# One inverse root for eight pairs of tiles, and no negated mean, in the main loop of a cross-attention and ternary feed-forward kernel

## What is computed

```python
x = x + xattn(layernorm(x), ctx_1024, Wq, Wk, Wv, Wo)   # x: (64, 512, 512), ctx: (64, 77, 512)
x = x + ffn(layernorm(x), weight, bias)
# layernorm: (x - m) / sqrt(v + eps), no learned scale
# xattn: 16 query heads of 32 summed to 4 key heads, rope on q and k, softmax over 77,
#        out.mean over the 4 heads, then @ Wo
# ffn: ternary weight; i_scale = max|x| / 127 over the whole input, x rounded to -128..127, matmul, scales, bias
```

## Time and profile before

| | us |
|---|---|
| median of 3 runs | 1320.01 (1319.31 to 1321.22) |
| the profiled execution, its own time | 1319.5 |
| its span in the profile | 1317.7 |
| busy time: PE, PEld | 1267.9, 1085.9 |
| busy time: DVE, ACT, POOL | 1181.8, 1025.1, 791.2 |

### The profile page before, as it was taken

The page is one execution under the profiler, slowest core; times in us unless marked ns, Lnnn a source line. Parts: engine busy times, 40 slices in busy tenths (PEclk is TensorE's granted clock), DMA queues, the critical chain, the costliest instruction groups (busy, mean ns, idle before and its releaser), DMA issues.

```text
span 1317.7 us, 36811 instructions
## 1 busy us (share of the span) xinstructions
PE 1267.9 (96%) x9848; PEld 1085.9 (82%) x9911; DVE 1181.8 (90%) x2772; ACT 1025.1 (78%) x2338; POOL 791.2 (60%) x1536
## 2 busy tenths in 40 slices
PE   5897999999999999999999999999969999999998
PEld 5796999999999999999999999999935555555554
DVE  4876899999999999999999999999978888888887
ACT  3454788888888888888888888888857878888886
POOL 3564888888888888888888888888820000000000
PEclk9999999999999999999999999999979999999999
DMA  8574355555555555555546452323108999999945
GB/s 266 166 216 133 107 158 182 154 183 161 176 165 171 165 171 167 170 171 166 178 159 187 150 169 76 102 80 98 37 5 332 400 401 395 401 399 404 406 201 223
DMA packets 100815, 265.18 MB, mean 201 GB/s; under 512 B 49705, under 2 KB 65769, under 8 KB 72114
## 3 DMA queue, kind: packets, MB, share of 16 engines
q1 hardware_dynamic: 100786, 264.86, 58.8%
HBM read 139.64 MB, written 125.17 MB: 201 GB/s over the span
## 4 chain that ended last, share of the span: by engine, by line
DVE 47%; PE 31%; issue 15%; DMA 2%; DVEq 2%; SPq 1%; ACT 1%; POOL 1%; POOLq 0%; ACTq 0%
PE bank L1248 18%; DVE amax L898 10%; DVE x_sb L930 8%; DVE e_sb L944 6%; DVE mx_sb L940 5%; DVE bn_sb L889 5%; PE bank L1239 4%; PE bank L1246 3%; DVE qT_sb L912 2%; PE bank L1065 2%; DVE rinv_sb L886 2%; DVE ve_sb L918 2%; DVE bn_sb L881 2%; DVE mv_sb L904 1%; DMA x_sb<-in_ctx 1%
## 5 line engine op out<-in xcount | busy, mean ns | idle before, releaser
L1248 PE MATMUL bank<-wT,x_sb 128*128 128x512 f16 x1024 | 263.9, 380 | 3.5 <-issue 0.2
L1168 PE MATMUL bank<-wqs,xT_sb 128*128 128x128 f32 x2048 | 259.7, 280 | 0.2
L718 ACT ACTIVATE x_sb<-bank,mean,cols 128x512 f32<-128x512 f32 x256 | 196.0, 774 | 67.6 <-PE bank L1248 67.3
L1168 PEld LDWEIGHTS bank<-wqs,xT_sb 128*128 128x128 f32 x2048 | 238.2, 191 | 7.1 <-ACT xT_sb L640 0.8
L1216 PE MATMUL bank<-v_blk,pT_sb 103*128 103x136 f32 x1536 | 199.0, 279 | 0.3 <-ACT pT_sb L682 0.3
L1216 PEld LDWEIGHTS bank<-v_blk,pT_sb 103*128 103x128 f32 x1536 | 190.6, 190 | 0.5 <-ACT pT_sb L682 0.5
L1248 PEld LDWEIGHTS bank<-wT,x_sb 128*128 128x128 f16 x1024 | 100.5, 98 | 106.8 <-issue 1.6
L930 DVE SCALAR_TENSOR_TENSOR x_sb<-x_sb,negm,bank 128x512 f32 (+1 forms) x256 | 179.5, 742 | 7.9 <-PE bank L1179 2.7
L898 DVE TENSOR_REDUCE amax<-x_sb (+1 forms) x128 | 156.0, 1218 | 23.2 <-DVE bn_sb L889 8.0
L691 ACT ACTIVATE sq_sb<-x_sb 128x512 bf16 (+1 forms) x256 | 161.4, 631 | 18.7 <-DVE x_sb L930 1.4
L1005 DVE TENSOR_TENSOR x_sb<-x_sb 128x512 f32 (+1 forms) x256 | 164.5, 683 | 1.2 <-ACT x_sb L718 1.2
(11 more groups left out here) (126 smaller groups left out, 2584.4 us busy)
## 6 DMA issues: line engine op xcount, KB each, us to landing
out_y<-x_sb SPq DMA_DIRECT2D x112, 1024.0 KB, 7.2
x_sb<-in_x SPq DMA_DIRECT2D x64, 1024.0 KB, 6.5
x_sb<-out_y SPq DMA_DIRECT2D x48, 1024.0 KB, 9.0
x_sb<-in_ctx SPq DMA_DIRECT2D x38, 256.0 KB, 2.8
k_blk<-k_scr SPq DMA_DIRECT2D x256, 19.2 KB, 5.5
k_scr<-x_sb SPq DMA_DIRECT2D x38, 128.0 KB, 2.3
v_scr<-x_sb SPq DMA_DIRECT2D x38, 68.0 KB, 2.3
v_blk<-v_scr SPq DMA_DIRECT2D x128, 10.2 KB
```

What stands on the lines that cost most here:

```text
L718: act.activation(u_sb[:, t, :], bank[4 + t][:, :], ACT.Identity, bias=stat_of(mean1, j, t, back), scale=cols[:, 6:7]).then_inc(scaled_t, 1)
L1168: last = pe.matmul(bank[2][:, t * HD:(t + 1) * HD], xT_sb[:, t, c, :], wqs[:, c, :], start=c == 0, stop=c == EC - 1)
L1248: last = pe.matmul(bank[4 + t][:, :], q16T_sb[:, t, c, :], wT[:, c, :], start=False, stop=c == EC - 1)
```

## The change

Three things change.

1. The second inverse root is no longer taken in every step. `ve2_sb` grows from two buffers of 2 columns to one of 16, and in the step in which the eighth pair of a group reaches RSTD, DVE forms 16 variances in one instruction and POOL raises 16 columns to the power -1/2 in one instruction. That happens 16 times: 15 times in step k = 5 of the loop's rounds and once in the drain's last step. The constant `mhalf` becomes 16 columns wide. DVE waits for the group before instead of the pair before, and the scalar section waits for 16 increments instead of 128.
2. `negm` is gone. The mean stays in `mv_sb`, which gets a place for each of the eight pairs, and its three readers take it from there: the residual add subtracts it, and POOL adds it.
3. `stats_ready` is raised once a pair, not twice.

```diff
-        mv_sb = sb("mv_sb", [P, 2, 2])
+        mv_sb = sb("mv_sb", [P, UN, 2, 2])
-        ve2_sb = sb("ve2_sb", [P, 2, 2])
-        negm = sb("negm", [P, UN, 2])
+        ve2_sb = sb("ve2_sb", [P, 2 * UN])
-        mhalf = sb("mhalf", [P, 2])
+        mhalf = sb("mhalf", [P, 2 * UN])
...
 # POOL
-                if rstd:
+                if rstd and rstd[1] == UN - 1:
                     j, kj, gj = rstd
-                    pool.wait_ge(var_ready, j + 1)
-                    pool.tensor_tensor(rs2[:, bass.ds(2 * j, 2)], ve2_sb[:, kj % 2, :], mhalf[:, :], ALU.pow)\
+                    pool.wait_ge(var_ready, gj + 1)
+                    pool.tensor_tensor(rs2[:, bass.ds(2 * UN * gj, 2 * UN)], ve2_sb[:, :], mhalf[:, :], ALU.pow)\
                         .then_inc(rs2_ready, 1)
...
-                    pool.wait_ge(stats_ready, 2 * j + 2)
-                    pool.tensor_tensor(rs_sb[:, kj, :], ve_sb[:, kj % 4, :], mhalf[:, :], ALU.pow)\
+                    pool.wait_ge(stats_ready, j + 1)
+                    pool.tensor_tensor(rs_sb[:, kj, :], ve_sb[:, kj % 4, :], mhalf[:, 0:2], ALU.pow)\
...
-                    pool.tensor_tensor(mean1[:, bass.ds(2 * j, 2)], o_sb[:, :, D], negm[:, kj, :],
-                                       ALU.subtract).then_inc(mean_ready, 1)
+                    pool.tensor_tensor(mean1[:, bass.ds(2 * j, 2)], o_sb[:, :, D], mv_sb[:, kj, :, 0],
+                                       ALU.add).then_inc(mean_ready, 1)
...
 # DVE
-                if rstd:
+                if rstd and rstd[1] == UN - 1:
                     j, kj, gj = rstd
-                    if not resid:
-                        dve.wait_ge(rs2_ready, j - 1)
+                    at_least(dve, rs2_ready, gj)
                     dve.wait_ge(sq_done, 2 * j + 2)
-                    dve.tensor_scalar(ve2_sb[:, kj % 2, :], ssq[:, bass.ds(2 * j, 2)], 1.0 / E, EPS, ALU.mult, ALU.add)\
-                       .then_inc(var_ready, 1)
+                    dve.tensor_scalar(ve2_sb[:, :], ssq[:, bass.ds(2 * UN * gj, 2 * UN)], 1.0 / E, EPS,
+                                      ALU.mult, ALU.add).then_inc(var_ready, 1)
...
-                        dve.bn_aggr(mv_sb[:, t, :], bn_sb[:, t, :]).then_inc(mv_ready, 1)
+                        dve.bn_aggr(mv_sb[:, kj, t, :], bn_sb[:, t, :]).then_inc(mv_ready, 1)
...
-                    dve.tensor_scalar(ve_sb[:, kj % 4, :], mv_sb[:, :, 1], float(D), D * EPS, ALU.mult, ALU.add)\
-                       .then_inc(stats_ready, 1)
-                    dve.tensor_scalar(negm[:, kj, :], mv_sb[:, :, 0], -1.0, None, ALU.mult)\
+                    dve.tensor_scalar(ve_sb[:, kj % 4, :], mv_sb[:, kj, :, 1], float(D), D * EPS, ALU.mult, ALU.add)\
                        .then_inc(stats_ready, 1)
...
-                                                 scalar=negm[:, kj, t:t + 1], in1=bank[t][:, :],
-                                                 op0=ALU.add, op1=ALU.add).then_inc(added_t, 1)
+                                                 scalar=mv_sb[:, kj, t, 0:1], in1=bank[t][:, :],
+                                                 op0=ALU.subtract, op1=ALU.add).then_inc(added_t, 1)
...
-            dve.wait_ge(rs2_ready, NP_)
+            dve.wait_ge(rs2_ready, GRP)
```

## The result

The changed kernel is slower: 1342.69 us (1342.49 to 1346.15, 6 runs) against 1319.66 us (1317.41 to 1322.25, 6 runs) for the kernel before; the ratio is 1.0181 with a 95% interval of 1.0164 to 1.0198. The medians are 23.0 us apart. The forecast was 1363 us in a range of 1319 to 1370 us. The profiled execution took 1342.8 us, 23.3 us more than that of before (1319.5 us).

The account below looks back on a forecast made before the run. PE was taken to bound the loop at 6.55 us a step. Stalls of 40.2 us plus 3.2 for the last root less 0.26 make 43.1 on 1319.5, with 0.5 for the median 1363 us; range 1319 to 1370.

Parts of the forecast that it names:

- What paces the loop: Main loop: PE sets the pace at 6.55 us a step; DVE has at least 0.25 us of slack in each.
- the quick step of 6.30 us: DVE's shortest step at one round's end, when it made good a delay; taken as within its reach.
- PE's spacing below 6.5 us: Loop: the prediction is wrong if PE's steps get this close where DVE has less to do.
- DVE's removed instructions, at nothing: Loop: dropping the negated mean and seven of eight second variances saves 0.23 us a step on DVE, hidden by PE.
- The 29.6 us: Loop: the gain over 128 steps if DVE is the bound and the width nearly free, 1290 us; chance 0.08.
- The stall, C - 1.22 us: Every eighth loop step: PE waits for the rope behind the long root beyond 1.22 us of slack; 2.7 us, fifteen times.
- The root's duration C: POOL's 16-column inverse root: 0.70 us plus 14 columns at 0.23 us, 3.9 us; by-the-column case 3.5 to 4.3, chance 0.45.
- the upper bound: 16-column root on POOL: all excess over a plain operation goes by the column, 0.256 us each, 4.29 us in all.
- the cost lies between: Rival on the 16-column root: half the upper slope, 2.5 us long, 21 us lost, 1341 us; chance 0.20.
- the four cases: Root costs by the column 0.45, in between 0.20, nearly free 0.27, DVE as bound 0.08; range holds the first three.
- the formula: Whole kernel: 15 x (C - 1.22) in the loop, plus C - 0.70 for the last root, less 0.26 us; 43.1 us.
- the 0.26 us of the forecast: Drain: POOL starts the last head step earlier without an inverse root in front, so PE gets `ost_sb` 0.26 us sooner.

Follow-up runs that it names:

- e1_no_negm: The kernel before with only the negated mean removed, one 2-column inverse root a pair kept; 1318.96 us, ratio 0.9993.
- e6_no_loop_roots: The changed kernel without the second inverse root and its variance in the loop, only the drain's group computed; 1321.31 us, ratio 1.0013.
- e9_dve_plus_2: The kernel before with two more DVE instructions a step, copies of the negated mean that nothing reads; 1318.80 us, ratio 0.9986.
- e8_four_pairs_after_rope: The changed kernel with one 8-column root for four pairs, moved behind the rope in POOL's step; 1318.04 us, ratio 0.9980.
- e10_dve_plus_6: The kernel before with six more DVE instructions a step, copies of the negated mean that nothing reads; 1382.34 us, ratio 1.0465.

## Why the prediction was right, and where it was off

**What paces the loop: right.** It rested on PE's even spacing while DVE was late. The experiments confirm it from both sides: less DVE work (`e1_no_negm`, `e6_no_loop_roots`) brings nothing, a little more (`e9_dve_plus_2`) costs nothing, and DVE's floor of 6.27 us lies where the quick step of 6.30 us put it. That PE doesn't notice DVE's lateness holds to some 0.02 us: at most turns of before its projections are 6.56 or 6.57 us apart, in `e9_dve_plus_2`, with more work on DVE, 6.54 to 6.55 us. PE's spacing below 6.5 us was named as a sign of being wrong, and 6.47 us occurs once a round. But that step always comes behind a stall, and without stalls no step falls below 6.53 us in `e6_no_loop_roots`, where DVE has less to do as well.

**DVE's removed instructions, at nothing: right.** The 29.6 us at the other end of that term were never there to have. They were also reckoned too high: the 0.17 us from the negated mean to the next instruction holds some waiting, and where DVE is late, at the turn in the trace of before, the two start 0.08 us apart (535.64 and 535.72).

**The stall, C - 1.22 us: right.** With the C measured, 2.91 us, it gives 1.69 us, and the spacing shows 1.66. It holds at 1.65 us (0.43 reckoned, 0.33 to 0.40 seen) and at 1.02 us (none). That the wait is at L1146, that one stall covers everything behind the root and that POOL is back in time one step later are all in the timeline.

**The root's duration C: mis-sized.** This is the step that failed in its amount. I took 0.23 us a column, nine tenths of the upper bound, on the ground that no set-up could take the 0.51 us by which the 2-column root exceeds a plain operation. The measured slope is 0.158 us, so 0.32 of the 0.51 us go by the column and 0.2 us are a set-up of the power's own. C is 2.91 us, not 3.9, and the forecast of 43 us of loss became 23. The case "the cost lies between" (0.13 us a column, 1341 us), which I gave 0.20, came nearest. The time lay within the range all the same, but a range of 51 us that holds three of the four cases says little; what the experiments bear out is the formula and not the size put into it. The loop over elements that the Trainium skill describes (GPSIMD Engine Reference, Instruction dispatch) is what the widths show. Its fixed part is larger here, 0.39 us for a power and 0.19 us for an add, than that rule's tens of cycles made me believe.

**The sum.** With the measured C the formula gives 15 x 1.69 + 2.21 - 0.26 = 27.3 us, and the profiled executions differ by 23.3. From the first to the last projection the loop is (966.97 - 115.82) - (945.29 - 115.90) = 21.8 us longer, not 25.4: a round loses 1.52 us (53.92 - 52.40), because PE gives 0.07 us back in the step behind a stall and keeps 6.54 us instead of 6.55 in the rest, and the first steps of the two executions differ by about 1 us besides; of this 0.56 us is the first scores' wait for the DMA of `k_blk`, 1.22 us after and 1.78 us before. From the last projection to L958 it is 26.78 - 25.44 = 1.34 us longer, where 1.95 were reckoned. There the drain gained 0.87 us, not 0.26. First, 0.35 us up to the last transposes of `ost_sb`, which start 18.61 us after the last projection instead of 18.96; the 0.26 us of the forecast belong here. Second, 0.26 us up to the output projection behind them (L1175, L1179 before), as the two transposes run in 0.44 us instead of 0.69. Third, 0.29 us up to DVE's residual add, as that projection takes 0.94 us instead of 1.22. The last two go with TensorE's granted clock, 1.00 for its higher level of 2.4 GHz and 0.50 for the lower of 1.2: after, it is 1.00 between 984 and 986 us and 0.71 in the two behind; before, it had fallen to 0.85 between 962 and 964 us, where PE was busy for 0.32 us, and was 0.50 from 964 on. The forecast had no term for this. What makes the projection behind a stall 0.08 us shorter was not tried.

## What to carry to other kernels

Before work is put together into one long instruction on an engine that others wait for, price the long one by the column: a short instruction in every step can lie in the slack that a long one in one step of eight overflows, even where the sum of the long ones is half that of the short ones. The slack is found from the engine that paces, as the time between the end of what it needs and its start, plus what the feeding engine idles before; place and length of the new instruction add up against it. To see which of two nearly full engines paces, look for a place where one of them is late by itself, and see whether the other notices.

## What was not expected

The power on GpSimd costs 158 ns a column here (from 2 to 32 columns of 128 rows in fp32), 80 times an add's 2 ns, over a fixed 0.39 us.

Kernels with the same loop differ by more than their intervals say: `e9_dve_plus_2`, with more work than the kernel before, has a ratio of 0.9986 (0.9977 to 0.9995), and `e6_no_loop_roots`, with less, 1.0013 (1.0004 to 1.0022). So 0.15% either way is not an edit's doing here, and the 0.2% of `e8_four_pairs_after_rope` is too near to it to be called a gain; of the profile's evidence only the loop's 6.54 us a step speaks for it, since from the last projection to the scalar section it takes 26.03 us, more than the 25.44 of before. Part of the spread sits in the first steps: the third projection starts 5.41 us after the second in the profiled execution of the changed kernel, 5.98 us in that of before and 8.61 us in that of `e9_dve_plus_2`, where the first scores wait for the DMA of `k_blk` and the granted clock is 0.50 from 123 to 130 us. What makes these executions start differently was not tried.

At each turn of the hardware loop DVE idles in front of its maximum, 0.51 us in the kernel before and 0.42 us in `e10_dve_plus_6`. It costs nothing while DVE has slack; in `e10_dve_plus_6`, where it has none, the turn costs 0.8 us a round, about half by this pause. Its cause was not tried.
